# Attention on one core: row scores, shift transposes and output transposes share a ring of three PSUM banks, all four row passes of two steps run behind the scores, and GpSimd masks the diagonal probabilities

## The chip, the cores and the metric

The program runs on one core of a Trainium2 chip. The metric is the device time of one execution in microseconds (us), lower is better. The whole program is a layer of causal attention, a time-mixing layer (RWKV) and two expert layers; the change lies in the attention alone.

The engines are named as the profile names them: PE is TensorE (PEld its weight loads), DVE is VectorE, ACT is ScalarE, POOL is GpSimd, SP is SyncE, which issues DMAs.

## The reference

The part that the change touches is plain causal attention with 16 heads of 32 columns over 2048 rows:

```python
qkv = jnp.einsum('bsd,od->bso', x, w_project)          # x: 1 x 2048 x 512
q, k, v = ...                                          # 16 heads of 32
att = jnp.einsum('bhqd,bhkd->bhqk', q, k) / math.sqrt(HEAD_DIM)
att = jnp.where(causal, -1e9, att)                     # causal: above the diagonal
att = jax.nn.softmax(att, axis=-1)
out = jnp.einsum('bhqk,bhkd->bhqd', att, v)
return jnp.einsum('bsd,od->bso', out.transpose(...).reshape(b, s, d), w_out)
```

## The kernel before, in words

`stage_attention` works on two heads at a time (HPAIR), eight pairs of heads (`pair(n, i, ...)`: pair 0, then a loop of three turns with two pairs each, then pair 7). For each head the queries and keys lie as stacks of a high and a low part, 96 rows deep, so that the products of scores keep their precision (`q_stack`, `k_stack`). Two sets of stacks take turns; SP loads the next pair's set when the set is free.

Each pair does the scores twice, in two directions:

- **Row passes** (`rows_unit`, L598): 128 queries on the partitions, up to 512 keys in the free direction. They serve only to find each query's maximum, which DVE takes from PSUM (`reduce_unit`, L540). There are 40 steps in a pair (`row_steps`), with one pass for each of the two heads in each. A pass that ends at the diagonal has a second one behind it (L601) that adds the mask as a product of an identity and a mask matrix in bf16.
- **Score passes** (`scores`, L621): 128 keys on the partitions, up to 512 queries in the free direction, again 40 steps with two heads (`steps`: four query blocks j of 512, and for each the key tiles kt from 0 to its diagonal). 16 of the 40 steps touch the diagonal, with widths of 512, 384, 256 and 128. There a mask pass in bf16 follows each score pass (L624, `mask_t`). ACT takes the exponential of both heads at once (L514) from one of two double banks (`p_cols`) into one of four buffers (`probs`).
- **Products** (`products`, L636): the values times the probabilities, summed in the bank `p_out` over the steps of a query block. They are in plain f32, two passes for each head, the heads side by side.

The maximum enters the scores as two extra rows of the query stack. When the rows of a query block are all reduced, DVE puts their maxima into `shift` (L545 to L551), PE turns it (`turn_shift`, L611), ACT copies the result out of PSUM (`copy_shift`, L500), and SP sends it to DRAM and back into the rows of the stack (`move_shift`). This happens at the steps 22, 30, 2 and 18 of a pair (`shift_at`), the first two for the next pair. The row passes run 22 steps ahead of the scores (LEAD); before the first pair 22 steps of them fill the lead.

The output of a query block is copied out of `p_out` by ACT (`copy_out`, L504), turned by PE in four transposes (`turn_out`, L647) at the steps 7, 15, 27 and 3 (`turn_at`, the last for the pair before), and divided by its sums by DVE into `heads` (`block_out`, L556 and L559).

PSUM has eight banks here: two for rows (`p_rows`), four for scores (`p_cols`), one for outputs (`p_out`) and one that both kinds of transposes share (`p_turn`). The order on every engine is the order in which the code is written. On PE a step issues its scores, the row pass of the first head, on every second step the products of the two steps before, the row pass of the second head, and then a transpose if one is due:

```python
scores(n, i, m)
if more:
    rows_unit(pn, pi, row, 0)
if m % 2 == 1:
    for before in (m - LAG - 1, m - LAG):
        ...products...
if more:
    rows_unit(pn, pi, row, 1)
```

On ACT the copy of a shift comes behind the exponential of the step after the transpose; on DVE the output of a block comes behind the two reductions of the step after the transpose, which is the first step of the next two.

## Time and profile before

| what | us |
|---|---|
| median of three timed runs | 3827.97 |
| the three runs | 3811.81, 3827.97, 3828.18 |
| the profiled execution | 3811.86 |
| span of the profiled execution | 3809.6 |
| busy in the span: PE, DVE, ACT, POOL | 3370.4, 2097.7, 1584.8, 1089.8 |
| first row pass of the attention to the last product into `heads` | 181.3 to 906 |

The span is one execution from its first to its last instruction. Busy times are of the whole program. The profiler models the ends of matmuls, so PE's busy time is that of records and overlaps its own idle time a little; the distance from one start to the next is the better measure of what a pass costs. PEclk is the clock that TensorE was granted, as a share of 2.4 GHz. A time in square brackets in a timeline row is the idle time of that engine before the row, with what ended it.

### The profile page before, as it was taken

To read this page: it belongs to the slowest core of one execution; us is meant where nothing else is said; L and a number is where in the kernel's file an instruction comes from. 1 tells how busy PE (TensorE), PEld (TensorE's weight loads), DVE (VectorE), ACT (ScalarE), POOL (GpSimd) and SP (SyncE) were. 2 spreads that over 40 slices of the span, in tenths; PEclk is the share of its full clock that TensorE was granted. 3 is DMA by queue.
4 is the path that set the end of the run, shared out by engine and by line. 5 is a ranking of instruction groups with operands and counts; after the bars stand their busy time and mean duration, and the time that the engine had idled before them with its cause. 6 is when DMAs were issued, how large, how long until landed. Compare 5 with 4: busy or idle time off the path is not lost. (4 is left out here: it accounts for less than half of the span.)

```text
span 3809.6 us, 61820 instructions
## 1 busy us (share of the span) xinstructions
PE 3370.4 (88%) x16308; PEld 2533.8 (67%) x16309; DVE 2097.7 (55%) x3549; ACT 1584.8 (42%) x2090; POOL 1089.8 (29%) x841
## 2 busy tenths in 40 slices
PE   7899999999788879999999958858887999998996
PEld 6644444444565668888888823327655888888886
DVE  4265555551465455555555558766553555555554
ACT  2134444443210145555555555522011555555553
POOL 0100000000223234444444423312232444444443
PEclk9889999999698989999999978977888999999998
DMA  4501111201300056666665520032002566665554
GB/s 166 146 10 35 35 36 43 51 9 56 107 23 12 17 176 165 162 150 166 167 168 147 101 102 22 23 120 78 19 12 98 158 165 166 169 157 148 145 145 104
DMA packets 108270, 379.03 MB, mean 99 GB/s; under 512 B 14000, under 2 KB 14768, under 8 KB 96176
## 3 DMA queue, kind: packets, MB, share of 16 engines
q1 hardware_dynamic: 55536, 253.66, 19.9%
q0 software_dynamic: 52608, 123.76, 16.9%
q8 instruction: 71, 1.16, 0.1%
q14 instruction: 55, 0.45, 0.0%
HBM read 277.49 MB, written 104.07 MB: 100 GB/s over the span
## 5 line engine op out<-in xcount | busy, mean ns | idle before, releaser
L1522 DVE TENSOR_TENSOR g_lo<-g_raw,g_hi x232 | 562.8, 2426 | 431.3 <-ACT g_hi L1469 393.4
L1424 POOL DMA_INDIRECT acc_rows<-g_y,g_ids x232 | 411.8, 1775 | 876.6 <-DVE g_ids L1532 367.1
L1469 ACT ACTIVATE g_hi<-g_raw x232 | 469.7, 2025 | 431.5 <-issue 325.8
L540 DVE TENSOR_REDUCE b_part_max<-b_p_rows 128x1 f32<-128x512 f32 (+3 forms) x640 | 375.0, 609 | 307.2 <-PE b_p_rows L601 154.4
L514 ACT ACTIVATE b_probs<-b_p_cols 128x1024 f32<-128x1024 f32 (+1 forms) x320 | 282.4, 898 | 385.5 <-PE b_p_cols L621 199.4
L1415 POOL DMA_INDIRECT g_rows_in<-xn_rows,g_ids x240 | 337.2, 1405 | 88.6 <-issue 88.0
L1574 PE MATMUL g_p_gate<-g_hi,g_rows_hi 128*128 x928 | 324.3, 349 | 37.6 <-issue 27.5
L1574 PE MATMUL g_p_gate<-g_hi,g_rows_lo 128*128 x928 | 303.6, 327 | 0.0
L1574 PE MATMUL g_p_gate<-g_lo,g_rows_hi 128*128 x928 | 303.5, 327 | 0.0
L598 PE MATMUL b_p_rows<-b_k_stack,b_q_stack 96*128 96x512 f32 (+3 forms) x640 | 275.7, 458 | 30.0 <-DMA b_k_stack<-qk_hi 18.5
L1574 PE MATMUL g_p_up<-g_hi,g_rows_hi 128*128 x928 | 299.0, 322 | 0.0
L1574 PE MATMUL g_p_up<-g_lo,g_rows_hi 128*128 x928 | 298.6, 322 | 0.0
L1574 PE MATMUL g_p_up<-g_hi,g_rows_lo 128*128 x928 | 298.2, 321 | 0.0
L1589 PE MATMUL g_p_y<-g_hi,g_hidden_hi 128*128 (+1 forms) x696 | 276.0, 397 | 10.8 <-issue 10.8
L1589 PE MATMUL g_p_y<-g_lo,g_hidden_hi 128*128 (+1 forms) x696 | 276.2, 397 | 0.0
L636 PE MATMUL b_p_out<-b_probs,b_v_pair 128*64 128x512 f32 (+3 forms) x1280 | 273.7, 549 | 0.0
L1589 PE MATMUL g_p_y<-g_hi,g_hidden_lo 128*128 (+1 forms) x696 | 273.1, 392 | 0.0
L598 PEld LDWEIGHTS b_p_rows<-b_k_stack,b_q_stack 96*128 96x128 f32 x640 | 126.8, 201 | 195.8 <-DVE b_part_max L540 90.5
L1456 ACT ACTIVATE g_gate<-g_p_gate 128x352 f32<-128x352 f32 x232 | 108.3, 467 | 284.2 <-PE g_p_gate L1574 274.4
L621 PE MATMUL b_p_cols<-b_q_stack,b_k_stack 98*128 98x512 f32 (+3 forms) x640 | 214.5, 409 | 3.6 <-issue 3.5
L1574 PEld LDWEIGHTS g_p_gate<-g_hi,g_rows_hi 128*128 128x128 f32 x928 | 177.6, 191 | 57.8 <-issue 56.6
L1006 ACT ACTIVATE f_gate<-f_p_mm 128x512 f32<-128x512 f32 x40 | 24.0, 599 | 394.1 <-PE f_p_mm L1279 394.1
(315 smaller groups left out, 6743.8 us busy)
## 6 DMA issues: line engine op xcount, KB each, us to landing
g_raw<-in_expert_weights_dram SPq DMA_DIRECT2D x64, 2176.0 KB, 8.9
acc_rows<-f_acc SPq DMA_DIRECT2D x34, 256.0 KB, 2.0
qk_hi<-a_hi SPq DMA_DIRECT2D x32, 256.0 KB, 2.6
qk_lo<-a_lo SPq DMA_DIRECT2D x32, 256.0 KB, 2.9
b_q_stack<-qk_hi SPq DMA_DIRECT2D x32, 256.0 KB
b_k_stack<-qk_hi SPq DMA_DIRECT2D x32, 256.0 KB
xn_rows<-f_xn SPq DMA_DIRECT2D x8, 1024.0 KB, 5.5
a_x<-in_x_dram SPq DMA_DIRECT2D x4, 1024.0 KB
```

The lines of the kernel that those rows point to most:

```text
L514: act.activation(probs[:, q, :, 0:w], p_cols[:, m % NCOL, :, 0:w], ACT.Exp, scale=SCALE).then_inc(probs_ready, 1)
L540: v.tensor_reduce(part_max[:, h, t % BT, c:c + 1], p_rows[:, u % NROWB, 0:w], AX.X, ALU.max).then_inc(rows_free, 1)
L598: mm = pe.matmul(p_rows[:, u % NROWB, 0:w], q_stack[i][h][0:NPART, t * P:(t + 1) * P], k_stack[i][h][0:NPART, c * BW:c * BW + w], start=Tr ...
L621: mm = pe.matmul(p_cols[:, m % NCOL, h, 0:BW - d], k_stack[i][h][0:NROW, kt * P:(kt + 1) * P], q_stack[i][h][0:NROW, j * BW + d:(j + 1) * ...
L636: mm = pe.matmul(p_out[h * HV:(h + 1) * HV, d:BW], v_pair[i][:, kt, h, :], probs[:, m % NPROB, h, 0:BW - d], start=(kt == 0), stop=(m in l ...
L1415: pool.indirect_dma_start(out=rows_in[:, i, :], out_offset=None, in_=xn_rows, in_offset=bass.IndirectOffsetOnAxis(ap=ids[:, i:i + 1].bitca ...
L1424: pool.indirect_dma_start(out=acc_rows, out_offset=bass.IndirectOffsetOnAxis(ap=ids[:, i:i + 1].bitcast(U32), axis=0), in_=y[:, n, :], in_ ...
L1456: act.activation(gate[:, i, :], p_gate[:, i, 0:M], ACT.Silu).then_inc(gate_ready, 1)
L1469: act.activation(hi[:, bass.ds(place, PIECE)], raw[:, bass.ds(source, PIECE)], ACT.Copy).then_inc(split_hi_ready, 1)
L1522: v.tensor_tensor(lo[:, bass.ds(place, PIECE)], raw[:, bass.ds(source, PIECE)], hi[:, bass.ds(place, PIECE)].bitcast(F32), ALU.subtract).t ...
L1574: m = pe.matmul(p_g[:, i, 0:M], x[:, i, c, :], w[:, bass.ds(at + (c * 2 + g) * M, M)], start=(n == 0), stop=(n == len(parts) - 1))
L1589: m = pe.matmul(p_y[:, i, :], x[0:z, i, c, :], w[0:z, bass.ds(at + UP + c * D, D)], start=(n == 0), stop=(n == len(parts) - 1))
```

## The change

The two banks of rows and the bank of transposes become one ring of three banks, `p_ring`. Every row pass, every shift transpose and every out transpose takes the next bank of the ring, in the order in which PE issues them. `fill_order` and `pair_order` write this order down, `bank` gives the bank, and `wait_ring` makes PE wait until the operation three places before has been released: a row pass by DVE's reduction (`rows_free`), a shift transpose by ACT's copy (`shift_copied`), an out transpose by DVE's product into `heads` (`turned_free`). PE works in blocks of two steps: the scores of both, a shift transpose if one is due, all four row passes, an out transpose if one is due, then the products of the two steps before. The orders on DVE and ACT stay as they are.

The mask passes on the scores (L624, `mask_t`) are gone. In their place POOL sets the probabilities above the diagonal to 0 in `probs` after the exponential, and the products of the 16 diagonal steps wait for POOL. The mask passes on the rows stay. SP starts the load of the second set of stacks when the first has landed.

```diff
-    NPROB, NCOL, NROWB = 4, 2, 2
+    NPROB, NCOL, NRING = 4, 2, 3
...
+    pair_order = []
+    for m in range(0, NSTEP, 2):
+        if m in shift_at:
+            pair_order.append(("shift", m, shift_at[m][0]))
+        pair_order += [("row", m, h) for h in range(HPAIR)]
+        pair_order += [("row", m + 1, h) for h in range(HPAIR)]
+        if m + 1 in turn_at:
+            pair_order.append(("out", m + 1, turn_at[m + 1][0]))
...
-        p_rows = s.enter_context(nc.psum_tensor("b_p_rows", [P, NROWB, BW], F32))
+        p_ring = s.enter_context(nc.psum_tensor("b_p_ring", [P, NRING, BW], F32))
...
-        p_turn = s.enter_context(nc.psum_tensor("b_p_turn", [P, BW], F32))
...
+                    for m in DIAGONAL:
+                        pool.wait_ge(probs_ready, n * NSTEP + m + 1)
+                        pool.sem_inc(mask_order, 1)
+                        pool.affine_select(out=probs[:, m % NPROB, :, 0:P], in_=probs[:, m % NPROB, :, 0:P], compare_op=ALU.is_ge, fill=0.0,
+                                           base=0, pattern=[[0, HPAIR], [1, P]], channel_multiplier=-1).then_inc(masked, 1)
+                        if m == last_step[0] and not is_last(n):
+                            if not is_first(n):
+                                pool.wait_ge(probs_free, n * NSTEP + NPROB)
+                            take_values(n + 1, 1 - i)
...
                         load_stacks(0, 0)
+                        sp.wait_ge(loaded[0], LOADED)
                         load_stacks(1, 1)
...
+                def wait_ring(n, kind, m, x=0):
+                    at = pair_at[kind, m, x] - NRING
+                    while at >= 0 and skipped(n, *pair_order[at][:2]):
+                        at -= NRING
+                    if at >= 0:
+                        wait_released(n, *pair_order[at])
...
-                        if kt >= j * BT:
-                            mm = pe.matmul(p_cols[:, m % NCOL, h, 0:P], ident_b[:], mask_t[:], start=False, stop=True)
...
-                    pe.wait_ge(probs_ready, n * NSTEP + m + 1)
+                    if m in DIAGONAL:
+                        pe.wait_ge(masked, n * len(DIAGONAL) + DIAGONAL.index(m) + 1)
+                    else:
+                        pe.wait_ge(probs_ready, n * NSTEP + m + 1)
...
+                    for m in range(0, NSTEP, 2):
                         scores(n, i, m)
+                        scores(n, i, m + 1)
+                        if m in shift_at and not skipped(n, "shift", m):
+                            j, ahead = shift_at[m]
+                            wait_ring(n, "shift", m)
+                            turn_shift(n + 1 if ahead else n, j, bank("shift", m))
+                        rows_ahead(m)
+                        rows_ahead(m + 1)
+                        if m + 1 in turn_at and not skipped(n, "out", m + 1):
+                            j, behind = turn_at[m + 1]
+                            wait_ring(n, "out", m + 1)
+                            turn_out(n - 1 if behind else n, j, bank("out", m + 1))
+                        for before in (m - LAG, m - LAG + 1):
+                            if before >= 0:
+                                products(n, i, before)
```

What this moves on PE is best read from the order of its instructions. In the rows below, names of waits are those of an earlier stage whose semaphore numbers this stage uses again. The first place is the out transpose of a pair in the loop, at step 7. Before, `a_ident_ready` is `rows_free`:

```order
L598 MATMUL b_p_rows<-b_k_stack,b_q_stack 128x512 [waits a_ident_ready]
L636 MATMUL b_p_out<-b_probs,b_v_pair 64x512 [waits a_product,a_lo_ready]
L636 MATMUL b_p_out<-b_probs,b_v_pair 64x512
L636 MATMUL b_p_out<-b_probs,b_v_pair 64x512 [waits a_product]
L636 MATMUL b_p_out<-b_probs,b_v_pair 64x512
L596 REGISTER_ALU
L598 MATMUL b_p_rows<-b_k_stack,b_q_stack 128x512 [waits a_ident_ready]
L647 MATMUL b_p_turn<-ident,b_out_t 128x128 [waits a_stored0,a_xT_hi_ready,a_lo_ready]
L647 MATMUL b_p_turn<-ident,b_out_t 128x128 x3
L619 REGISTER_ALU
L621 MATMUL b_p_cols<-b_q_stack,b_k_stack 128x512 [waits a_product]
```

Now the transposes stand behind all four row passes, and the products of two steps behind them. `a_stored0` is `out_free`, `a_normed` is `rows_free`:

```order
L654 MATMUL b_p_ring<-b_k_stack,b_q_stack 128x512 [waits a_normed]
L625 REGISTER_ALU
L695 MATMUL b_p_ring<-ident,b_out_t 128x128 [waits a_stored0,a_normed]
L695 MATMUL b_p_ring<-ident,b_out_t 128x128 x3
L688 MATMUL b_p_out<-b_probs,b_v_pair 64x512 [waits a_lo_ready,a_stored0]
L688 MATMUL b_p_out<-b_probs,b_v_pair 64x512
L688 MATMUL b_p_out<-b_probs,b_v_pair 64x512 [waits a_lo_ready]
L688 MATMUL b_p_out<-b_probs,b_v_pair 64x512
L670 REGISTER_ALU
L672 MATMUL b_p_cols<-b_q_stack,b_k_stack 128x512 [waits a_lo_ready]
```

The row passes of the next block, a little further on, with `a_stored2` for `turned_free`, the release of the out transpose:

```order
L654 MATMUL b_p_ring<-b_k_stack,b_q_stack 128x512 [waits a_normed]
L625 REGISTER_ALU
L654 MATMUL b_p_ring<-b_k_stack,b_q_stack 128x512 [waits a_normed]
L654 MATMUL b_p_ring<-b_k_stack,b_q_stack 128x256 [waits a_stored2]
L657 MATMUL b_p_ring<-b_mask,b_ident 128x128
L625 REGISTER_ALU
L654 MATMUL b_p_ring<-b_k_stack,b_q_stack 128x256 [waits a_normed]
L657 MATMUL b_p_ring<-b_mask,b_ident 128x128
```

So the third row pass behind an out transpose waits until DVE has emptied the transpose's bank. The second place is a shift transpose of the first pair, at step 18. `a_xT_hi_ready` is `shift_ready`, `a_w_hi_ready` is `shift_copied`. Before, it stood behind the row passes of its step and in a bank apart:

```order
L598 MATMUL b_p_rows<-b_k_stack,b_q_stack 128x128 [waits a_ident_ready]
L601 MATMUL b_p_rows<-b_mask,b_ident 128x128
L611 MATMUL b_p_turn<-ident,b_shift 128x128 [waits a_stored0,a_xT_hi_ready,a_normed]
L621 MATMUL b_p_cols<-b_q_stack,b_k_stack 128x512 [waits a_product]
L621 MATMUL b_p_cols<-b_q_stack,b_k_stack 128x512
L598 MATMUL b_p_rows<-b_k_stack,b_q_stack 128x256 [waits a_ident_ready]
```

Now:

```order
L662 MATMUL b_p_ring<-ident,b_shift 128x128 [waits a_xT_hi_ready,a_normed]
L654 MATMUL b_p_ring<-b_k_stack,b_q_stack 128x128 [waits a_normed,a_x_loaded1]
L657 MATMUL b_p_ring<-b_mask,b_ident 128x128
L654 MATMUL b_p_ring<-b_k_stack,b_q_stack 128x128 [waits a_normed]
L657 MATMUL b_p_ring<-b_mask,b_ident 128x128
L654 MATMUL b_p_ring<-b_k_stack,b_q_stack 128x256 [waits a_w_hi_ready]
```

It stands behind the scores and ahead of the row passes, and the third row pass behind it waits for ACT's copy.

## Rows read from the trace of the kernel before

**Rows 1.** Busy time by stretch: count, clock, DMA share, GB/s; filling, one pair.
```profile
181.30:212.90 31.60, 29.37 (x68) 15.52 (x69) 24.10 (x48) 1.82 (x3) 0.00 (x0) 0.50 0.44 89
...
301.48:387.07 85.59, 83.57 (x407) 42.43 (x405) 50.52 (x100) 38.35 (x48) 1.04 (x1) 1.00 0.18 39
```

**Rows 2.** Waits, 213 to 905 us: total, times, longest.
```profile
PEld b_p_rows L598 <- DVE b_part_max L540: 78.7, 191, 0.8
```

**Rows 3.** Timeline of PE, five blocks of pair 1: start, length, what, count.
```profile
356.26 0.71 PE L621 MATMUL b_p_cols<-b_q_stack,b_k_stack 98*128 98x512 f32 x2
...
361.02 0.71 PE L621 MATMUL b_p_cols<-b_q_stack,b_k_stack 98*128 98x512 f32 x2
...
365.50 0.71 PE L621 MATMUL b_p_cols<-b_q_stack,b_k_stack 98*128 98x512 f32 x2
...
367.74 0.47 PE L598 MATMUL b_p_rows<-b_k_stack,b_q_stack 96*128 96x512 f32 x1
368.14 1.94 PE L636 MATMUL b_p_out<-b_probs,b_v_pair 128*64 128x512 f32 x8
...
370.34 0.63 PE L621 MATMUL b_p_cols<-b_q_stack,b_k_stack 98*128 98x512 f32 x2
...
372.04 0.39 PE L598 MATMUL b_p_rows<-b_k_stack,b_q_stack 96*128 96x512 f32 x1
372.36 1.94 PE L636 MATMUL b_p_out<-b_probs,b_v_pair 128*64 128x512 f32 x8
374.23 0.50 PE L598 MATMUL b_p_rows<-b_k_stack,b_q_stack 96*128 96x512 f32 x1
374.56 0.64 PE L621 MATMUL b_p_cols<-b_q_stack,b_k_stack 98*128 98x512 f32 x2
375.04 0.98 PE L598 MATMUL b_p_rows<-b_k_stack,b_q_stack 96*128 96x512 f32 x2
...
378.74 0.47 PE L621 MATMUL b_p_cols<-b_q_stack,b_k_stack 98*128 98x512 f32 x1
```

**Rows 4.** Timeline of PE, a score pass with its mask in pair 2.
```profile
387.69 0.47 PE L621 MATMUL b_p_cols<-b_q_stack,b_k_stack 98*128 98x512 f32 x1
388.01 0.23 PE L624 MATMUL b_p_cols<-b_mask_t,b_ident 128*128 128x128 bf16 x1
388.05 0.80 PE L598 MATMUL b_p_rows<-b_k_stack,b_q_stack 96*128 96x512 f32 x2
```

**Rows 5.** Groups of POOL by form: a select, a copy.
```profile
L440 POOL COPY b_v_pair<-values 128x1024 f32 x6 | 6.3, 1042 | 566.0 <-PE b_p_out L636 566.0
...
L146 POOL TENSOR_SCALAR_AFFINE_SELECT ident<-ident 128x128 f32<-128x128 f32 x1 | 0.3, 287 | 0.2 <-POOL ident L144 0.2
```

**Rows 6.** Timeline of DVE, the same blocks of pair 1.
```profile
363.20 0.20 DVE L556 RECIPROCAL b_recip<-b_p_turn 128x8 f32<-128x8 f32 x1
363.55 0.42 DVE L559 TENSOR_TENSOR heads<-b_p_turn,b_recip 128x256 f32 x1
...
366.96 1.97 DVE L540 TENSOR_REDUCE b_part_max<-b_p_rows 128x1 f32<-128x512 f32 x3
...
372.47 0.69 DVE L540 TENSOR_REDUCE b_part_max<-b_p_rows 128x1 f32<-128x512 f32 x1 [0.45 <-PE b_p_rows L598]
```

**Rows 7.** Timeline of ACT, the block with a shift transpose.
```profile
367.94 1.02 ACT L514 ACTIVATE b_probs<-b_p_cols 128x1024 f32<-128x1024 f32 x1 [0.67 <-PE b_p_cols L621]
368.86 0.25 ACT L500 ACTIVATE b_shift_t<-b_p_turn 16x128 f32<-16x128 f32 x1
```

**Rows 8.** Timeline of PE from pair 3 to 4, and the clock's stretch.
```profile
474.88 0.50 PE L621 MATMUL b_p_cols<-b_q_stack,b_k_stack 98*128 98x512 f32 x1 [1.73 <-issue]
477.51 0.27 PE L624 MATMUL b_p_cols<-b_mask_t,b_ident 128*128 128x128 bf16 x1 [2.13 <-issue]
...
566.46 0.40 PE L621 MATMUL b_p_cols<-b_q_stack,b_k_stack 98*128 98x512 f32 x1
...
477.50:487.80 10.30, 10.29 (x37) 6.07 (x38) 5.17 (x10) 3.57 (x6) 1.04 (x1) 0.50 0.42 91
```

More of the change, by code:

```diff
@@ L351, in stage_attention @@
     assert max(shift_at) + 1 < NSTEP and max(turn_at) + 1 < NSTEP
-    shifts_by = lambda m: sum(x <= m for x in shift_at) + 2
-    turns_by = lambda m: sum(x < m for x in turn_at) - 1
+    assert all(m % 2 == 0 for m in shift_at) and all(m % 2 == 1 for m in turn_at)
+    fill_order = []
+    for m in range(LEAD):
+        fill_order += [("row", m, h) for h in range(HPAIR)]
+        if m - 1 in last_step:
+            fill_order.append(("shift", m, last_step.index(m - 1)))
+    pair_order = []
[6 more added lines that the diff above has]
+            pair_order.append(("out", m + 1, turn_at[m + 1][0]))
+    pair_order.append(("out", NSTEP, NB - 1))
+    fill_at = {(kind, m, x if kind == "row" else 0): at for at, (kind, m, x) in enumerate(fill_order)}
+    pair_at = {(kind, m, x if kind == "row" else 0): at for at, (kind, m, x) in enumerate(pair_order)}
+    STRIDE = -(-(len(pair_order) - 1) // NRING) * NRING
     with ExitStack() as s:
@@ L417, in is_last, with skipped, bank @@
             return isinstance(n, int) and n == NPAIR - 1
+        def skipped(n, kind, m):
+            if kind == "out":
+                return m == NSTEP and not is_last(n) or m < NSTEP and turn_at[m][1] and is_first(n)
+            return is_last(n) and (m + LEAD >= NSTEP if kind == "row" else shift_at[m][1])
+        def bank(kind, m, x=0, filling=False):
+            return (fill_at if filling else pair_at)[kind, m, x] % NRING
         with nc.Block() as block:
@@ L507, in pair @@
                     if is_first(n):
-                        copy_shift(0, 0)
-                        copy_shift(0, 1)
+                        for j in range(2):
+                            copy_shift(0, j, bank("shift", last_step[j] + 1, filling=True))
                     for m in range(NSTEP):
@@ L551, in block_shift, with block_out @@
                     v.tensor_tensor(shift[:, 1, :], neg_max[:], shift[:, 0, :], ALU.subtract).then_inc(shift_ready, 1)
-                def block_out(n, j):
+                def block_out(n, j, ring):
                     o = n * NB + j
+                    if not (isinstance(n, int) and o == 0):
+                        v.wait_ge(turned_free, o)
+                    turned_out = p_ring[:, ring, :].rearrange("p (t h c) -> p t h c", t=BT, h=HPAIR)
                     v.wait_ge(out_turned, o + 1)
@@ L565, in pair @@
                             for h in range(HPAIR):
-                                reduce_unit(0, m, h)
+                                reduce_unit(0, m, h, bank("row", m, h, filling=True))
                             if m in last_step:
@@ L572, in pair @@
                             for h in range(HPAIR):
-                                reduce_unit(n + 1 if ahead else n, (m + LEAD) % NSTEP, h)
+                                reduce_unit(n + 1 if ahead else n, (m + LEAD) % NSTEP, h, bank("row", m, h))
                             if m in max_at:
@@ L590, in _, with wait_released @@
                 pe.sem_inc(probs_free, NPROB)
-                def rows_unit(n, i, m, h):
+                def wait_released(n, kind, m, x):
+                    if kind == "row":
+                        ahead = m + LEAD >= NSTEP
+                        unit = (m + LEAD) % NSTEP * HPAIR + x
+                        pe.wait_ge(rows_free, (n + 1 if ahead else n) * NSTEP * HPAIR + unit + 1)
+                    elif kind == "shift":
+                        pe.wait_ge(shift_copied, (n + 1 if shift_at[m][1] else n) * NB + x + 1)
+                    else:
+                        pe.wait_ge(turned_free, (n - 1 if m < NSTEP and turn_at[m][1] else n) * NB + x + 1)
@@ new lines, in wait_filling @@
+                def wait_filling(at):
+                    kind, m, x = fill_order[at]
+                    if kind == "row":
+                        pe.wait_ge(rows_free, m * HPAIR + x + 1)
+                    else:
+                        pe.wait_ge(shift_copied, x + 1)
+                def wait_ring(n, kind, m, x=0):
[4 more added lines that the diff above has]
+                        wait_released(n, *pair_order[at])
+                    elif is_first(n):
+                        wait_filling(max(f for f in range(len(fill_order)) if f % NRING == at % NRING))
+                    else:
+                        last = max(f for f in range(STRIDE) if f % NRING == at % NRING and f < len(pair_order) - 1)
+                        wait_released(n - 1, *pair_order[last])
@@ new lines, in pair, with rows_ahead @@
+                        for at, (kind, m, x) in enumerate(fill_order):
+                            if at >= NRING:
+                                wait_filling(at - NRING)
+                            if kind == "row":
+                                rows_unit(0, 0, m, x, at % NRING)
+                            else:
+                                turn_shift(0, x, at % NRING)
+                    def rows_ahead(m):
+                        ahead = m + LEAD >= NSTEP
+                        if ahead and is_last(n):
+                            return
+                        if m + LEAD == NSTEP:
+                            pe.wait_ge(loaded[1 - i], next_loads * LOADED)
+                        for h in range(HPAIR):
+                            wait_ring(n, "row", m, h)
+                            rows_unit(n + 1 if ahead else n, 1 - i if ahead else i, (m + LEAD) % NSTEP, h, bank("row", m, h))
```

97 lines of the change are left out of this document (27 added, 70 removed).

## The prediction

> **What bounds the kernel now.** I read the table of times first: one core, 3811.86 us of execution around a span of 3809.6 us. Of the timed runs two stand at 3828 us and the third, like the profiled one, at 3812. The change touches one stage only, the attention between 181 and 906 us, so all that counts is what this stage becomes; the other 3085 us are taken as they are.
>
> Second view, busy time by stretch [rows 1]. In one pair of heads (301.48 to 387.07, 85.6 us for 20 blocks of two steps) PE is busy 83.6 us, DVE 50.5, ACT 38.4, POOL 1.0. PE bounds the stage, and in it the sum of what it streams and of what it waits for. The list of waits [rows 2] says how little it waits: 78.7 us in 191 waits of a row pass for DVE's reduction of the pass two places before. This is where a third bank could help. The timeline of PE gives the prices [rows 3], over five blocks in a row. Passes of 512 behind each other start 0.24 us apart (two from 374.56 to 375.04); the first one behind the products has 0.33 us to itself (374.23 to 374.56). From the last row pass to the products are 0.40 us (367.74, 368.14), the products of two steps take 1.87 us (372.36 to 374.23). A block with an out transpose took 4.76 us (356.26 to 361.02), the one behind it 4.48 (to 365.50), one with a shift transpose 4.84 (to 370.34), two with neither 4.22 and 4.18 (to 378.74).
>
> **The change part by part.**
>
> *Masks on the scores go (256 of 512 mask passes).* A score pass of 512 with its mask starts its mask 0.32 us later and the next pass 0.04 us after that (387.69, 388.01, 388.05) [rows 4], where a bare pass takes 0.24: 0.12 us each, 32 in a pair, so 3.8 us a pair or some 30 us in all, on PE's path. Narrow passes give somewhat less, and the gain is inside the block times below.
>
> *POOL masks the probabilities instead.* 128 selects of 128x256 elements. The trace has a select of 128x128 at 0.287 us and a copy of 1024 elements a row at 1.04 us [rows 5]; I take 0.45 us, nearer to the select. A step's exponential ends 2.8 us into its block (worked out below), its products come a block later, 3 to 7 us into that, so the select has over 2 us to hide in even behind the narrow blocks. Price 0; were it 2 us long, I work out some 6 us for the stage. The copy of the next pair's values now lies between two selects, in front of steps whose products are 10 us off: 0.
>
> *All four row passes run behind four score passes, with three banks.* Now I count one block from its first score pass: scores at 0, 0.33, 0.57, 0.81, rows at 1.05, 1.29, 1.53. The fourth row pass takes the bank of the first. DVE starts 0.43 us behind a pass (372.04 on PE, 372.47 on DVE) and takes 0.69 alone and 0.66 in a run [rows 6], so that bank is free at 2.2 us, not at 1.77: a new stall of 0.44. Then 0.40 to the products and 1.87 for them: **4.47 us**, against 4.18 before. The old order broke the run twice around the products, and stalled once as well; the new one saves one break and pays it back here. Blocks with masked scores gain 0.1 to 0.3, bare ones lose up to 0.27; over the nine blocks of a pair with no transpose in or just before them I make it 0.
>
> *A shift transpose takes a bank of the ring.* It stands before the rows (the last piece of the order shown); the third row pass behind it waits until ACT has copied it. ACT does so behind both exponentials of the block: the first starts 0.43 behind the second score pass, at 0.76, each takes 1.02, then 0.25 for the copy [rows 7]: 3.07 us. PE is in order, so the fourth pass and the products queue behind it, and DVE idles. The pass starts at 3.12 instead of 1.67; the fourth follows at 3.46, products at 3.86, end **5.73 us**, against 4.84: +0.9 in two blocks of a pair. In a third (steps 22, 23) the exponentials are short, and it gains 0.3. The transpose itself has nothing to wait for: its maxima come from the block before. Sum +1.5 a pair.
>
> *An out transpose takes a bank too.* In its own block it needs the second row's reduction (2.87 us), its four transposes cost 0.33 and 0.20, products and end at 3.4 and **5.27**, against 4.76: +0.5, four times. Behind it is the dear place. The third row pass of the next block takes its bank (third piece of the order shown, the wait on turned_free). DVE empties it only after it has reduced the first two rows of that next block: 1.05 + 0.43 + two reductions = 2.8, reciprocal and product 0.77 (363.20 to 363.97) [rows 6], so 3.64 us instead of 1.5, a stall of **2.1 us**. Rows with masks follow, products at 4.50, end **6.37**, against 4.48: +1.9, three times, and +1.5 where it falls on masked scores (steps 8, 9): 7.2 us a pair.
>
> *Sum of a pair:* 7.2 + 2.0 + 1.5 + 0 = **+10.7 us**. Six pairs have it; the first lacks one out transpose (+9.4), the last issues no row passes after step 17 (+5): **+79 us**.
>
> *Filling.* The first 44 row passes take 31.6 us for 24.1 us of DVE work [rows 1], at 1.2 GHz granted. With three banks DVE runs nearly through: 26.5 us, **-5 us**, between -7 and 0.
>
> *The load waits.* SP now starts the second set of stacks when the first has landed. While the filling runs, DMA moves 31.6 us x 89 GB/s = 2.8 MB [rows 1], most of the second set (12 loads of 256 KB, 3.1 MB). So the first set came first already, and the second is wanted only at step 18 of the first pair, some 40 us into the scores: 0.
>
> *Clock.* The granted clock is 1.00 (2.4 GHz) in the pair of rows 1 and 0.50 (1.2 GHz) for 10.3 us behind two idle times of PE, 1.73 us before 474.88 and 2.13 us before 477.51, where the loop turns [rows 8]. That pair runs from 474.88 to 566.46, 91.6 us where an undisturbed one has 85.6; less the 2.1 us of idle time, 3.9 us a fall. The new stalls of 2.1 us are as long, though alone. I put two or three falls into the sum, +8 us, with 0 and the rival below as ends.
>
> **Sum:** 3811.9 + 79 - 5 + 8 = 3894 us against the profiled execution. Executions of before lie at 3812 and 3828, so I take the middle, 3820, and forecast **3902 us**; against the median shown (3828) the same sum gives 3910.
>
> **Rivals.**
>
> *The clock swings (0.17).* Every full pair has four stalls of 2.1 us and two of 1.4, 30 of the long ones in all. For it: the fall behind 474.88 [rows 8]. Against: that fall had two such idle times in a row. If it falls at every second of the 30 long stalls, 15 times, and costs 3 us since a slower PE waits less in the ring, it is +45 in place of +8: 3820 + 79 - 5 + 45 = 3939 us; at every stall 3984. The Trainium skill, "TensorE: Matmul & The Clock Gate", section "A second HAM failure mode: psum-queue depth-cycling", has this very picture, a kernel cycling through PSUM banks whose small idle times make the clock swing. By that rule the time is the 3939 us of this rival, without it the 3894 of the sum; the trace agrees only so far that idle time is what the clock falls after.
>
> *The ring does not bite (0.07, other side).* If turned banks came free before the third row pass, 1.5 us into a block, none of the long stalls would be there. The price is then masks (-30) and the row waits of today (a third of 78.7) without new ones: some 55 us off, 3765 us. It decides at DVE: its out pair must go ahead of the two reductions. The order of DVE is unchanged, with the pair behind them, and PE's third pass waits on exactly that count; so only an error in my reading of the order makes this come true.
>
> *Gains and stalls cancel (0.06).* A third bank takes more of today's waits than I see, and stalls are half as long: +79 becomes within 19 of 0, 3820 us.
>
> *The select is slow (0.05, inside the range).* Over 2 us, products wait for POOL: +6 to +20.
>
> **How the numbers follow.** The forecast with small errors holds 0.65, all cases together 1. A measurement of this kernel tells 0.5% (19 us) from no change. The rival of the other side is the 0.07 for faster, the cancelling one the 0.06 for the same, and the rest, 0.87, is slower. The low end, 3866, is the sum with all stalls a fifth shorter and no fall of the clock, from 3812 (3811.9 + 63 - 7 = 3868). The high end, 3960, is stalls a tenth longer and the clock rival in part. Left out: faster, same, and the clock falling at every stall.
>
> **What would show it.** Right: a pair of heads takes 96 us; the waits of row passes for DVE grow from 79 to over 110 us, and a new wait of a row pass for DVE's product into heads appears some 30 times at about 2 us, and one for ACT's shift copy at 1.4; the reductions still take 0.69. POOL at 0.45 us a select with nobody waiting. PE's busy share of the pair falls, its granted clock stays near 1.0. Wrong: blocks behind an out transpose under 5 us, or the clock under 0.9 through the stage, or PE waiting for POOL.

## The result, and the profile after

The changed kernel takes **3911.56 us** (median; four runs, 3905.86 to 3922.66) against 3822.11 for the kernel before in the same job (3811.81 to 3828.18): a ratio of 1.024 [1.0204, 1.0277], 89 us slower. The prediction was 3902 with 3866 to 3960 around it. The profiled execution took 3908.42 us.

The page, its engines and three groups (columns as on the page):

```profile
span 3906.4 us, 61705 instructions
...
PE 3363.5 (86%) x16050; PEld 2527.1 (65%) x16053; DVE 2077.8 (53%) x3549; ACT 1570.8 (40%) x2090; POOL 1142.5 (29%) x968
...
L567 DVE TENSOR_REDUCE b_part_max<-b_p_ring 128x1 f32<-128x512 f32 (+3 forms) x640 | 352.0, 604 | 413.3 <-PE b_p_ring L654 279.4
...
L654 PE MATMUL b_p_ring<-b_k_stack,b_q_stack 96*128 96x512 f32 (+3 forms) x640 | 229.0, 435 | 114.4 <-DVE heads L589 54.5
...
L469 POOL TENSOR_SCALAR_AFFINE_SELECT b_probs<-b_probs 128x256 f32<-128x256 f32 x128 | 50.8, 408 | 755.8 <-ACT b_probs L541 755.5
```

PE's busy time differs from that of before by 7 us, yet the span is 97 us longer: the time went into waiting. Row passes stood idle for 114.4 us, and the largest releaser is new, DVE's product into `heads`. POOL's select takes 0.408 us, and POOL sits waiting for ACT. Hardly anybody waits for POOL: in the stage 9 weight loads of products do, for 2.2 us in all, none longer than 0.3.

Busy time by stretch, in the columns of [rows 1]: the filling, pair 1 (the pair after the first, as in [rows 1]), and the stage from the first scores on:

```profile
307.00:406.00 99.00, 85.01 (x374) 42.27 (x372) 48.15 (x100) 36.61 (x48) 7.32 (x17) 0.95 0.16 33
181.10:207.10 26.00, 24.84 (x68) 15.28 (x69) 22.80 (x49) 1.82 (x3) 0.00 (x0) 0.50 0.58 123
...
207.10:993.00 785.90, 678.70 (x2909) 336.81 (x2908) 362.33 (x750) 292.50 (x382) 57.69 (x135) 0.93 0.12 26
```

The pair takes 99.0 us where it took 85.6, the filling 26.0 in place of 31.6. Of the 99.0 us PE is idle for 14.0; it was 2.0. The granted clock of the pair is 0.95, not 1.00: the stretches at 0.50 (1.2 GHz) are short and many. Two of them, and the same length behind the first:

```profile
349.60:353.00 3.40, 3.40 (x10) 1.09 (x7) 0.95 (x4) 0.00 (x0) 0.00 (x0) 0.50 0.00 0
250.60:254.00 3.40, 3.40 (x10) 1.06 (x7) 1.09 (x4) 0.00 (x0) 0.00 (x0) 0.50 0.00 0
353.00:356.40 3.40, 2.13 (x14) 1.48 (x14) 1.02 (x4) 2.08 (x3) 0.00 (x0) 1.00 0.01 2
```

Between the first scores and the last block there are 25 stretches at 0.50, 102.4 us in all: 22 of 3.4 us, one of 6.8 and two of 10.2. The kernel before has 2 (23.9 us, both where the loop turns).

Waits from 210 to 985 us (engine, line, waited for: total, times, longest), against [rows 2]:

```profile
PEld b_p_ring L654 <- DVE heads L589: 67.5, 30, 2.3
PE b_p_ring L654 <- DVE heads L589: 54.5, 30, 1.9
PEld b_p_ring L654 <- DVE b_part_max L567: 47.6, 90, 0.8
...
PEld b_p_ring L654 <- ACT b_shift_t L527: 28.9, 29, 1.6
...
PE b_p_ring L654 <- ACT b_shift_t L527: 19.0, 21, 1.3
```

The waits for reductions fell from 78.7 to 47.6 us; the third bank did that. The turned banks put 67.5 and 28.9 us beside them. How the new wait comes about stands in the timelines of a block with an out transpose and the one behind it, in pair 2. PE:

```profile
443.32 0.51 PE L654 MATMUL b_p_ring<-b_k_stack,b_q_stack 96*128 96x512 f32 x1 [0.31 <-DVE b_part_max L567]
443.92 0.65 PE L695 MATMUL b_p_ring<-ident,b_out_t 128*128 128x128 f32 x4
444.50 1.94 PE L688 MATMUL b_p_out<-b_probs,b_v_pair 128*64 128x512 f32 x8
446.37 1.19 PE L672 MATMUL b_p_cols<-b_q_stack,b_k_stack 98*128 98x512 f32 x4
447.40 0.62 PE L654 MATMUL b_p_ring<-b_k_stack,b_q_stack 96*128 96x512 f32 x2
449.86 0.50 PE L654 MATMUL b_p_ring<-b_k_stack,b_q_stack 96*128 96x512 f32 x1 [1.84 <-DVE heads L589]
...
450.73 1.94 PE L688 MATMUL b_p_out<-b_probs,b_v_pair 128*64 128x512 f32 x8
...
453.63 0.27 PE L662 MATMUL b_p_ring<-ident,b_shift 128*128 128x128 f32 x1
...
455.49 0.38 PE L654 MATMUL b_p_ring<-b_k_stack,b_q_stack 96*128 96x256 f32 x1 [1.27 <-ACT b_shift_t L527]
```

DVE in the same time:

```profile
447.83 1.29 DVE L567 TENSOR_REDUCE b_part_max<-b_p_ring 128x1 f32<-128x512 f32 x2 [2.78 <-PE b_p_ring L654]
449.04 0.20 DVE L586 RECIPROCAL b_recip<-b_p_ring 128x8 f32<-128x8 f32 x1
449.38 0.42 DVE L589 TENSOR_TENSOR heads<-b_p_ring,b_recip 128x256 f32 x1
```

The transposes are done by 444.57. DVE idles 2.78 us with their bank full, because two reductions of passes that PE has not issued yet stand ahead of the product in its order; PE issues two and waits 1.84 us for the product behind them. ACT at the shift transpose:

```profile
453.37 1.94 ACT L541 ACTIVATE b_probs<-b_p_cols 128x1024 f32<-128x1024 f32 x2 [4.29 <-PE b_p_cols L672]
455.19 0.25 ACT L527 ACTIVATE b_shift_t<-b_p_ring 16x128 f32<-16x128 f32 x1
```

The copy waits its turn behind two exponentials that have nothing to do with it, and PE waits 1.27 us for the copy.

The blocks of pair 1 by kind, from one first score pass to the next (in brackets blocks of the same kind without a stretch at 0.50, from pair 2 or from a run below):

| steps | kind | before | predicted | after |
|---|---|---|---|---|
| 26, 27 | out transpose | 4.76 | 5.27 | 5.26 |
| 28, 29 | behind it | 4.48 | 6.37 | 7.86 (6.24) |
| 16, 17 | behind one | 4.49 | as above | 7.42 (6.23) |
| 8, 9 | behind one, masked scores | 4.51 | +1.5 | 5.91 |
| 4, 5 | behind one | 3.07 | +1.9 | 4.84 |
| 30, 31 | shift transpose | 4.84 | 5.73 | 5.43 |
| 18, 19 | shift transpose | 4.68 | as above | 7.20 (5.40) |
| 34, 35 | neither | 4.18 | 4.47 | 4.47 |
| the pair | | 85.6 | 96.2 | 99.0 |

### The profile page after: what moved, and what is told of

The parts are those of the page before. It is cut to its first block and busy times, and to the rows that moved or that the text cites. A ratio compares the mean times of both kernels' runs of the same rounds, so it can differ in the third digit from the quotient of the medians.

```text
span 3906.4 us, 61705 instructions
## 1 busy us (share of the span) xinstructions
PE 3363.5 (86%) x16050; PEld 2527.1 (65%) x16053; DVE 2077.8 (53%) x3549; ACT 1570.8 (40%) x2090; POOL 1142.5 (29%) x968
## 5 line engine op out<-in xcount | busy, mean ns | idle before, releaser
L567 DVE TENSOR_REDUCE b_part_max<-b_p_ring 128x1 f32<-128x512 f32 (+3 forms) x640 | 352.0, 604 | 413.3 <-PE b_p_ring L654 279.4
L541 ACT ACTIVATE b_probs<-b_p_cols 128x1024 f32<-128x1024 f32 (+1 forms) x320 | 269.2, 893 | 458.7 <-PE b_p_cols L672 457.5
L654 PE MATMUL b_p_ring<-b_k_stack,b_q_stack 96*128 96x512 f32 (+3 forms) x640 | 229.0, 435 | 114.4 <-DVE heads L589 54.5
L688 PE MATMUL b_p_out<-b_probs,b_v_pair 128*64 128x512 f32 (+3 forms) x1280 | 305.0, 603 | 0.0
L469 POOL TENSOR_SCALAR_AFFINE_SELECT b_probs<-b_probs 128x256 f32<-128x256 f32 x128 | 50.8, 408 | 755.8 <-ACT b_probs L541 755.5
L654 PEld LDWEIGHTS b_p_ring<-b_k_stack,b_q_stack 96*128 96x128 f32 x640 | 127.0, 204 | 180.1 <-DVE heads L589 67.5
L672 PEld LDWEIGHTS b_p_cols<-b_q_stack,b_k_stack 98*128 98x128 f32 x640 | 109.8, 200 | 135.0 <-issue 114.1
```

Of the source, the lines that this page charges most:

```text
L541: act.activation(probs[:, q, :, 0:w], p_cols[:, m % NCOL, :, 0:w], ACT.Exp, scale=SCALE).then_inc(probs_ready, 1)
L567: v.tensor_reduce(part_max[:, h, t % BT, c:c + 1], p_ring[:, ring, 0:w], AX.X, ALU.max).then_inc(rows_free, 1)
L654: mm = pe.matmul(p_ring[:, ring, 0:w], q_stack[i][h][0:NPART, t * P:(t + 1) * P], k_stack[i][h][0:NPART, c * BW:c * BW + w], start=True, s ...
L672: mm = pe.matmul(p_cols[:, m % NCOL, h, 0:BW - d], k_stack[i][h][0:NROW, kt * P:(kt + 1) * P], q_stack[i][h][0:NROW, j * BW + d:(j + 1) * ...
L688: mm = pe.matmul(p_out[h * HV:(h + 1) * HV, d:BW], v_pair[i][:, kt, h, :], probs[:, m % NPROB, h, 0:BW - d], start=(kt == 0), stop=(m in l ...
```

## The experiments

Theory T is the prediction's: turned banks make PE wait for DVE's and ACT's order. Its rivals: the clock takes the time, the order of PE does, or POOL does. All ratios are to the kernel before, timed in the same job as the run (3822 to 3824 us).

**One part alone: POOL masks the probabilities, everything else as before** (a_pool_mask_only).

```diff
-                            mm = pe.matmul(p_cols[:, m % NCOL, h, 0:P], ident_b[:], mask_t[:], start=False, stop=True)
...
+                        pool.affine_select(out=probs[:, m % NPROB, :, 0:P], in_=probs[:, m % NPROB, :, 0:P], ...
```

> The kernel before with one part of the change: POOL sets the probabilities above the diagonal to 0, and the mask passes on the scores go. Banks and order stay. Theory 1 (PE's order and waits decide): at most 0.12 us for each of 256 passes goes, 30 us, but where a row pass waits for its bank in the next breath the wait grows by what was saved, so 11 to 20 us faster, ratio 0.995 to 0.997; the waits of row passes for DVE grow from 79 to about 90 us. Theory 2 (every mask pass is on the path): 30 us faster, 0.992. If POOL's select delays the products: slower than before, with PE waiting for POOL.

Measured: 3809.75 us, 0.9964 [0.9952, 0.9976]. The waits of row passes for the reductions, to hold against [rows 2]:

```profile
PEld b_p_rows L602 <- DVE b_part_max L544: 105.6, 257, 0.8
```

Of some 30 us of mask passes 14 came back as time; the row waits grew by 27 us, from 78.7. With two banks of rows, PE arrived earlier at banks that were not free; the growth is more than twice what the expectation had. In the blocks of a pair the masks are worth little here: pair 1 takes 84.4 us in place of 85.6, so 1.2 us a pair and some 9 of the 14 us.

**The rest alone: the ring, with the masks on PE** (b_ring_pe_mask).

```diff
+                        if kt >= j * BT:
+                            mm = pe.matmul(p_cols[:, m % NCOL, h, 0:P], ident_b[:], mask_t[:], start=False, stop=True)
...
-                        pool.affine_select(out=probs[:, m % NPROB, :, 0:P], ...
```

> The changed kernel with the score masks back on PE and no selects on POOL; ring, order and load wait stay. Theory 1: the masks cost PE 16 us more than in the changed kernel, 3928 us, since they stand ahead of the rows and not in the shadow of a wait in most blocks; the long waits stay at 30 x 2 us. Theory 2: masks cost 30 us, 3942. If the long waits cover them: no change, 3912.

Measured: 3937.0 us, 1.0302 [1.0277, 1.0327]. That lies between the two theories. So the masks are worth 25 us of the changed kernel and the ring with its order costs some 113. The mask part is sound; everything that is lost is in the ring.

**DVE empties the transposes' bank first** (c_out_first): the same instructions, the product into `heads` ahead of two reductions.

```diff
                     for m in range(NSTEP):
+                        if m - 1 in turn_at:
+                            ...block_out(..., bank("out", m - 1))
                         for h in range(HPAIR):
                             reduce_unit(...)
-                        if m - 1 in turn_at:
-                            ...block_out(..., bank("out", m - 1))
```

> The changed kernel with one move on DVE: the reciprocal and the product into heads go ahead of the two reductions of the step behind the out transpose. Theory 1: the bank is free before the third row pass comes to it, so the 30 waits of 2 us for DVE's product go, 52 us, and with them the falls of the clock that follow them, some 30 us more: 3827 to 3860 us, blocks behind an out transpose at 4.4 to 4.6 in place of 5.9 to 7.8. Rival (the run of four row passes over three banks costs by itself, the turned banks are incidental): under 20 us, above 3890.

Measured: 3825.23 us, 1.0006 [0.9995, 1.0017]: **86 us of the 89 are gone**. DVE's timeline at the same transpose:

```profile
442.29 2.22 DVE L567 TENSOR_REDUCE b_part_max<-b_p_ring 128x1 f32<-128x512 f32 x4 [1.45 <-PE b_p_ring L654]
444.42 0.20 DVE L586 RECIPROCAL b_recip<-b_p_ring 128x8 f32<-128x8 f32 x1
444.76 0.42 DVE L589 TENSOR_TENSOR heads<-b_p_ring,b_recip 128x256 f32 x1
```

The product is done at 445.2, and the next block's scores begin at 446.1, so the bank is free before that block starts. Its pair 1:

```profile
297.40:385.10 87.70, 79.79 (x373) 41.35 (x373) 47.77 (x100) 36.61 (x48) 7.33 (x17) 1.00 0.18 38
```

The blocks behind an out transpose (steps 4, 8, 16 and 28) take 3.36, 4.37, 4.59 and 4.59 us, the wait for `heads` is no longer in the list, and the granted clock is back at 1.00, with one stretch at 0.50 in the stage in place of 25. The last point leaves open how much of the 86 us is the wait and how much the clock. The next run tells.

**The same wait, filled** (i_keep_busy): before each of the 30 waiting row passes PE adds 20 products of zeros to `p_out`, which change no value. The wait stays, but PE is busy in it.

```diff
+                                for _ in range(20):
+                                    pe.matmul(p_out[:, 0:P], zeros_b[:], ident_b[:], start=False, stop=False)
                             wait_ring(n, "row", m, h)
```

> The changed kernel with 20 small passes of zeros on PE (added to the output bank, so they add nothing) in front of each of the 30 row passes that wait for DVE's product into heads: 1.1 us of work in a wait of 2 us. Theory 1 with its clock part: the waits end when they ended before, but PE is not idle in them, the granted clock stays up, and 24 falls of 1 to 2 us go: 25 to 40 us faster than the changed kernel, some 3880 us. Rival (the falls cost nothing, since a slower PE only waits less): within 8 us of 3912. If the small passes delay the row passes: slower by up to 30 x 0.3 us.

Measured: 3884.35 us, 1.0155 [1.0132, 1.0178], 27 us faster with 600 more instructions. Its waits, and the stage by stretch:

```profile
PEld b_p_ring L654 <- DVE heads L589: 25.7, 30, 0.9
PE b_p_ring L654 <- DVE heads L589: 20.5, 30, 0.7
```

```profile
302.20:398.00 95.80, 86.30 (x454) 45.84 (x452) 48.14 (x100) 36.60 (x48) 7.29 (x17) 0.98 0.16 34
207.00:966.00 759.00, 685.98 (x3508) 363.31 (x3508) 362.03 (x750) 292.38 (x382) 57.45 (x135) 0.96 0.12 27
```

The blocks at steps 16 and 28 take 6.13 to 6.26 us, as long as an undisturbed one in the changed kernel (6.23), where most took 7.1 to 7.9; the filling changed their clock and not their wait. The stretches at 0.50 are 8 (47.8 us) in place of 25 (102.4): two at the turns of the loop, and six behind the wait for ACT's shift copy at step 18, which was not filled. Those behind a filled wait are all gone. The attention ends 26.9 us earlier for 17 fewer stretches: 1.6 us each. c_out_first removed 24, so at this price some 38 of its 86 us are clock and some 48 are wait, an estimate from the two runs. The clock swings because PE idles, not by itself.

**ACT copies the shift one exponential earlier** (d_shift_early).

```diff
-                        if m - 1 in shift_at:
-                            j, ahead = shift_at[m - 1]
+                        if m in shift_at:
+                            j, ahead = shift_at[m]
```

> The changed kernel with one move on ACT: the copy of a shift goes behind the first exponential of its block in place of the second. Theory 1: the third row pass behind a shift transpose waits about 1 us less in two blocks of a pair, 15 us in all, 3897 us; blocks with a shift transpose at steps 18 and 30 at 4.4 to 4.6 in place of 5.4. The waits for DVE's product into heads stay. Rival (these waits hide behind something else): no change, 3912.

Measured: 3899.42 us, 1.022 [1.018, 1.0261], 12 us faster by the medians. This interval overlaps that of the change, so the time alone does not decide; the wait and the blocks do. The wait, to hold against 28.9 us:

```profile
PEld b_p_ring L654 <- ACT b_shift_t L527: 14.2, 29, 0.7
```

The blocks of steps 18 and 30 take 4.49 and 4.62 us, where 5.40 and 5.43 stood: 1.7 us a pair, about 12 in all. e_both against c_out_first repeats the step: 15 us, with intervals that do not overlap.

**Both edits** (e_both).

```diff
+  the edit of c_out_first
+  the edit of d_shift_early
```

> The changed kernel with both moves, DVE's output pair ahead of the reductions and ACT's shift copy behind the first exponential. Theory 1: 15 us less than with DVE's move alone (3825), 3810 us, so about 0.3% faster than before; what is left is the fourth row pass that waits 0.4 us for the first reduction, some 130 times. If the two moves overlap: 3825.

Measured: 3809.73 us, 0.9975 [0.996, 0.9991], its pair 1 86.0 us. That is the time of a_pool_mask_only. With both stalls gone the third bank buys nothing yet: PE's own order, four row passes in one run, makes the fourth wait for DVE, as the next run shows.

**Both edits, and row passes again between the scores** (f_between): scores, two rows, scores, a shift transpose if due, two rows, products.

```diff
                         scores(n, i, m)
+                        rows_ahead(m)
                         scores(n, i, m + 1)
-                        rows_ahead(m)
                         rows_ahead(m + 1)
```

> Both moves, and on PE the two row passes of a step go behind the score passes of the same step (two scores, two rows, two scores, two rows, products). The passes stay one unbroken run of one kind, but the fourth row pass now comes 1.2 us behind the first and finds its bank free. Theory 1: another 0.44 us a block with all rows full, 6 us a pair, 45 to 50 us in all, 3762 us and 1.6% faster than before. Rival (the run is bound by DVE, which cannot reduce four passes of 0.66 us sooner wherever they stand): as without it, 3810.

Measured: 3756.57 us, 0.9838 [0.9816, 0.9859], 53 us faster than e_both. Pair 1 by stretch, and the waits that are left:

```profile
289.30:368.50 79.20, 77.88 (x373) 41.44 (x374) 47.95 (x100) 37.43 (x48) 7.49 (x17) 1.00 0.20 42
```

```profile
PEld b_p_ring L654 <- DVE b_part_max L567: 28.0, 76, 0.8
PE b_p_ring L654 <- DVE b_part_max L567: 4.7, 20, 0.3
```

PE is idle for 1.3 us of 79.2. Now the ring works: 28.0 us of waits for reductions against 78.7 with two banks.

**PE's order alone** (g_between_only): the changed kernel with that order, DVE and ACT as they were. It asks whether the run of four is a cause of its own.

```diff
                         scores(n, i, m)
+                        rows_ahead(m)
                         scores(n, i, m + 1)
-                        rows_ahead(m)
                         rows_ahead(m + 1)
```

> The changed kernel with only PE's order altered as two scores, two rows, two scores, two rows; DVE and ACT as in the changed kernel. Theory 1: the fourth pass's wait goes, and ACT and DVE release the turned banks relative to a third row pass that comes at much the same time, so the long waits for DVE's product into heads stay near 2 us: 3912 less 50 to 65, 3847 to 3862 us, still slower than before. Rival (the long waits need the run of four): at or under 3800.

Measured: 3830.11 us, 1.0028 [1.0015, 1.0041], 81 us faster than the change and outside both theories, 17 us faster than the first had it.

```profile
PEld b_p_ring L654 <- DVE heads L589: 53.4, 30, 1.8
PE b_p_ring L654 <- DVE heads L589: 41.4, 30, 1.5
```

The 30 waits for `heads` are there, each 0.4 us shorter, since the two score passes of a step now lie between the second row pass and the waiting third. The waits for the shift are gone (blocks of 3.91 and 4.64 us): only two row passes stand behind the shift transpose now, so its bank is next taken by the first row pass of the next block, behind the products. And the reductions are spread over the block. The clock still falls: 18 stretches at 0.50, 78.5 us, behind waits of 1.2 to 1.5 us on PE. The repairs are not additive: c_out_first alone takes 86 us off, this order alone 81, d_shift_early 12, which would make 179; all three (f_between) take 155.

**What the masks are worth in the best order** (k_between_pe_mask): f_between with the masks on PE.

```diff
+                            mm = pe.matmul(p_cols[:, m % NCOL, h, 0:P], ident_b[:], mask_t[:], start=False, stop=True)
-                        pool.affine_select(...)
```

> The best version so far (rows between the scores, both moves) with the score masks back on PE. Theory 1: with the waits of the ring gone, masks are worth what their passes take, 0.12 us at most for each of 256, 15 to 28 us: 3772 to 3785 us. Rival (worth no more than in the kernel before, where 14 us were measured): 3770.

Measured: 3787.82 us, 0.9912 [0.9896, 0.9928]: 31 us more than f_between. That is 0.12 us for each of the 256 passes, as in [rows 4], but by coincidence. The blocks say otherwise: pair 1 takes 81.95 us for 79.2, so 2.7 us a pair, 0.085 us a pass and some 22 us in all. The rest lies where the loop turns: with masks PE stops there a second time, ahead of the first mask pass (2.56 us at 460.64, as in [rows 8] before), and both turns have a stretch at 0.50 (10.2 and 13.7 us) where f_between has one of 10.2.

The same edit was worth 14 us with two banks, 25 in the changed kernel and 31 here. Block by block it is 1.2 us a pair with two banks, 0.4 to 0.5 us in each of seven blocks with masked scores in the changed kernel (some 3.2 a pair), and 2.7 here. So where a wait takes what a shorter stream gives, as with two banks, little is left; the order of 25 and 31 is not to be read from these times.

**The cover of POOL's select** (h_select_5x): five selects on the same data, each waiting for the one before; the values are the same.

```diff
-                        pool.affine_select(...).then_inc(masked, 1)
+                        for again in range(5):
+                            pool.affine_select(...).then_inc(selected, 1)
+                            pool.wait_ge(selected, ...)
+                        pool.sem_inc(masked, 1)
```

> The changed kernel with every select on POOL done five times over (the same values each time), 2 us and more in place of 0.41. Theory 1: the select is covered by the block between the exponential and its products, which is over 2 us long even in narrow blocks; at 2.1 to 2.4 us only the products behind the narrowest blocks wait, 5 to 15 us in all, 3917 to 3927. Rival (the masked products wait for POOL now): five times the cost shows fully, 128 x 1.7 us = 210 us, above 4100.

Measured: 4016.49 us, 1.052 [1.0502, 1.0537], 105 us more than the change: a miss for both theories. POOL's timeline at the first of the last four diagonal steps of pair 1 (step 36) and into the second, and PE's waits for it:

```profile
416.81 0.41 POOL L471 TENSOR_SCALAR_AFFINE_SELECT b_probs<-b_probs 128x256 f32<-128x256 f32 x1 [33.15 <-ACT b_probs L546]
417.38 0.41 POOL L471 TENSOR_SCALAR_AFFINE_SELECT b_probs<-b_probs 128x256 f32<-128x256 f32 x1 [0.16 <-POOL b_probs L471]
...
419.90 0.41 POOL L471 TENSOR_SCALAR_AFFINE_SELECT b_probs<-b_probs 128x256 f32<-128x256 f32 x1 [0.40 <-POOL b_probs L471]
```

```profile
PEld b_p_out L693 <- POOLq L475: 98.3, 59, 2.9
PE b_p_out L693 <- POOLq L475: 56.4, 49, 2.4
```

A masked step now takes POOL 3.09 us (416.81 to 419.90), not the 2.1 to 2.4 that the first theory reckoned with, and diagonal steps stand four in a row, eight where one pair ends and the next begins: 6.2 us for the two steps of a block that PE passes in 3.4 to 5.9 in the changed kernel. The queue of selects falls behind block by block. The cover of the select is thus the rate of two selects a block, not only the 2 us between an exponential and its products. The single select, 0.8 us a block, is far inside both. Not all of the 105 us is this queue: the stage has 38 stretches at 0.50 (249.2 us) in place of 25 (102.4), and the run does not separate the two.

**The load wait** (l_between_no_load_wait): f_between without SP's new wait.

```diff
-                        sp.wait_ge(loaded[0], LOADED)
```

> The best version so far without SP's wait ahead of the second set of stacks, so as it was before the change. Theory 1: the first set comes first anyway, so no change, 3757 us within 4. Rival (the first rows start earlier with the wait): 1 to 6 us slower.

Measured: 3755.24 us, 0.9826 [0.9809, 0.9843], against 3756.57: no difference outside the intervals, as the prediction had it.

**A version that beats both** (j_turn_between): f_between with the out transpose ahead of the last two row passes, and DVE's product ahead of that step's reductions.

```diff
-        pair_order += [("row", m + 1, h) for h in range(HPAIR)]
         if m + 1 in turn_at:
             pair_order.append(("out", m + 1, turn_at[m + 1][0]))
+        pair_order += [("row", m + 1, h) for h in range(HPAIR)]
```

> The best version so far with the out transpose ahead of the last two row passes of its block in place of behind them, and DVE's output pair one step earlier to match. Theory 1: the transpose no longer waits for the reduction of the second row pass (0.33 us), and neither does a row pass behind it, 4 times a pair, 8 to 12 us: 3746 us. Rival (the transpose costs by itself, four passes and the change of kind): no change, 3757.

Measured: **3750.72 us**, 0.9821 [0.9805, 0.9836]. Its pair 1 takes 78.5 us and its out-transpose blocks 4.65 for 4.80 in f_between. The interval overlaps that of f_between, so between these two the runs do not decide; both are 4% faster than the change and 1.6 to 1.8% faster than the kernel before.

## Why the prediction was right

The sum was made of the right mechanism; two of its terms were off in opposite directions and nearly cancelled. That the slowdown lies in the turned banks was foreseen; that 3902 came within 10 us of 3911.56 is in part luck.

*Where the time is.* In the profiled executions the attention ends at 993.4 us in place of 905.6, 87.8 us later; the sum said 82 (79 - 5 + 8). The code behind it is the same and took 2912.9 us in place of 2904.0; in the profiles of the experiments it took 2903 to 2928. No edit touches it; why it scatters is open.

*The turned banks.* "Behind it is the dear place": 30 waits for DVE's product, 1.8 us each on PE (forecast 2.1), the block behind a transpose at 6.24 (6.37). c_out_first shows that it decides: one move on DVE takes 86 us off. The shift's block was over-sized, 5.43 for 5.73. Without its three stretches at 0.50 pair 1 would take 99.0 - 1.2 - 1.8 - 1.6 = 94.4 us, +8.8 where the step said +10.7. The blocks behind give 6.7 of it (7.2 forecast), the out transposes 2.0 (2.0), the shifts 0.7 (1.5), the others -0.6 (0). Over the stage the 79 us are nearer to 64: the 88 measured, plus the 6 gained in the filling, less the 30 of clock (below). The block with neither transpose came out as worked out, 4.47.

*The clock.* "I put two or three falls into the sum, +8 us": this step failed. There were 25 stretches at 0.50, 22 of them of 3.4 us. 17 began in a wait for `heads` or within 2 us behind it, six behind the wait for the shift at step 18 (1.3 us), the other two within 7 us behind the turns of the loop. So 17 of the 30 long waits had one, nearly the rival's "every second of the 30 long stalls, 15 times": the rival was right in number and not in price. It said 3 us each; the blocks show 1.2 to 1.8 and i_keep_busy 1.6. Together that is about 38 us, less the 8 us that the two falls of before cost: 30 where 8 stood.

The price is small because the stretches are short. Half of 3.4 us is 1.7, an estimate of what PE loses in one at half the clock, and the blocks show about that; the 3.9 us worked out from the 10.3 us of [rows 8] were the price of a long stretch. A second error was to take the two idle times in a row of [rows 8] as what is needed. The length of one idle time does not tell either: 1.84 us at step 16 of pair 1 was followed by a stretch and 1.85 at step 8 was not, and the shift's waits of 1.3 us at step 18 were followed by one in six of seven cases in the changed kernel and in none in c_out_first. What decides is open.

The Trainium skill's rule in "TensorE: Matmul & The Clock Gate", "A second HAM failure mode: psum-queue depth-cycling", says that small idle times of PE between groups of matmuls that cycle through PSUM banks make its clock swing. The trace agrees: 102.4 us of the stage at 1.2 GHz, and 47.8 us once the idle times behind the out transposes are filled.

*The masks.* 30 us were forecast inside the block times, 25 measured here. The select's price of 0 held (0.41 us for 0.45), with 2.2 us of waits in all. The reason given for it, latency alone, was incomplete: the five selects show a queue that grows. They took 3.09 us a step, so the "6 us" for a select of 2 us was not tested.

*Filling and load.* 26.0 us for the 26.5 forecast, and a load wait of 0.

*What would show it.* Row waits for DVE "over 110": 67.5 + 47.6 = 115.1. One sign of a wrong picture, "blocks behind an out transpose under 5 us", was drawn too coarsely: the block at steps 4 and 5 takes 4.84 us, but it took 3.07 before, so it grew as forecast. About 30 waits at 2 us: 30, the longest 1.9 on PE. ACT's at 1.4: 1.3 the longest. Only the granted clock "near 1.0" was wrong, at 0.93 over the stage and 0.95 in the pair, above the bound of 0.9 that was named for a wrong picture and too low to call right. The low end of the range, 3866, is 2 us under the sum given for it, 3868; nothing hangs on that.

*The other side.* "It decides at DVE: its out pair must go ahead of the two reductions." c_out_first is that rival made true. It gives 3825 and not 3765, because the shift's stalls and the run of four passes are still there; with those gone too, f_between gives 3757. The rival named the right lever and took two obstacles too few into account.

## What to carry to other kernels

When producers of different kinds share a ring of buffers, the consumer's order must follow the producer's: for each slot look at which instruction frees it and at what stands in front of that instruction on its engine. If that is work that the producer has yet to issue behind the slot, the ring stalls; the one of three banks did so 30 times here, and other depths were not run. Put the release ahead of that work before adding a bank, then spread the users of the ring over other work; here that turned +2.4% into -1.8%. And what a removed instruction is worth is settled by what waits next to it: 1.2, 3.2 or 2.7 us a pair for the same mask passes. Read it from the blocks: whole times mix it with the clock and the turns of the loop.

## What the runs showed of the hardware

- Single idle times of PE were followed by short stretches at 1.2 GHz, mostly of 3.4 us, but not each of them: 17 of 30 waits of 1.7 to 1.9 us for `heads`, and six of the seven waits of 1.3 us for the shift at step 18. Each short stretch cost 1.2 to 1.8 us. In c_out_first none of the waits of 1.3 us was followed by one.
- Idle times of 1.7 to 2.6 us at the turns of the loop were mostly followed by a longer stretch at 1.2 GHz (10.2 and 13.7 us in the kernel before), and by none at one turn of c_out_first (2.50 us idle) and of f_between (1.81).
- Work of no use in place of idle time made a kernel faster: 600 small products, 27 us.
- A select of 128x256 on GpSimd takes 0.41 us, 0.57 from start to start when each waits for the one before by a semaphore of its own engine.
- The same program behind the attention differed by up to 24 us between profiled executions (2903 to 2928 us), so a span compares an edit in one stage less well than the end of that stage does.
